# Selective scan with C repeated by DMA and read on GpSimd, and weight splits spread over scan, gap and even cross groups

## The chip, the cores and the metric

The kernel runs on one core of one Trainium2 chip. The time is the device time of one execution in microseconds. Engines: PE is TensorE (PEld its weight loads), DVE is VectorE, ACT is ScalarE, POOL is GpSimd, SP is SyncE, whose queue issues all DMAs here. They run side by side and wait for one another through semaphores only.

## The reference

A two-layer decoder for x of shape (8, 128, 256). Layer 0: attention, a long convolution with ctx, a quantised feed-forward. Layer 1: a selective scan, a stage of self and cross attention with fp8 rounding ("cross" below), and a mixture of experts. The change touches the scan, cross and the start of the experts:

```python
# scan: D_STATE = 16
dt_x, B, C = split(einsum('bld,ed->ble', x, Wx), [64, 16, 16])
dt = softplus(einsum('blr,dr->bld', dt_x, Wdt) + bdt)
dA = exp(einsum('bld,dn->bldn', dt, -exp(A_log)))
dBx = einsum('bld,bln,bld->bldn', dt, B, x)
h = dA_t * h + dBx_t                       # over the 128 positions
y_t = einsum('bdn,bn->bd', h, C_t)         # sum over the 16 states
x = x + y + x * D
# cross: q, k, v, qx = fp8 linears of LN(x), per-head LN of q, k, qx
core = gqa(q, k, v);  xout = gqa(qx, kx, vx)   # kx, vx from ctx
x = x + einsum('bsi,oi->bso', fp8(concat(core, xout) / smooth), wproj) * scale
# experts: silu(h @ gate) * (h @ up) @ down, 16 routed (top 4) and a shared one
```

## The kernel before, in words

Each stage (`begin, attention, convolution, ffn, scan, cross, experts`) gives every engine a function, and each engine runs these one after another in written order. So an instruction waits for its semaphores and for all that its own queue holds ahead of it.

**Scan.** Channels lie on partitions in two halves c = 0, 1, and 8 x 128 = 1024 positions along the free axis. For each of the 16 states n and each c there is a step i = 2n + c. PE repeats the row B_n over all partitions into two PSUM banks (`spread`, a product with the one-column table `pick`), DVE multiplies it by `dtx` (L1114) and scans (L1118), ACT makes `dA`. The reading state x C_n is made by POOL for c = 0 (L1257, `read[0]`), from a copy of PE's spread of C_n that ACT takes out of PSUM (L1176, `c_copy`), and by DVE for c = 1 (L1123, `read[1]`), straight from PSUM. PE adds the readings up in PSUM by a product with the identity (`accumulate`, L1206).

**Splits.** The weights of cross are split into two float16 parts in chunks of 1024 columns: ACT scales a chunk into a scratch tile and casts it (L1409, L1411), POOL writes the remainder (L1417). All 26 chunks go in the first 26 steps of the scan, one a step: q, qx, k, v, the cross weights `kvx`, ctx and `side` (the output projection).

**Cross.** 32 groups g: two halves of the heads of each of 8 batches, first for the self path (g under 16, `path` 0), then for the cross path. For each group PE projects, turns, scores and mixes; DVE takes the maximum of the scores (`biggest`, L2079), divides, normalises (L2105), scales the output (`smoothed`, L2117) and rounds it to fp8 by three instructions (L2124, L1851, L1852); ACT squares, exponentiates (L2256) and copies (`take_pT` L2264, `take_turned` L2248); POOL takes roots (L2337), and adds and rounds (L2322, L2327). For the next batch ACT takes x (`take_x`, L2218), DVE quantises it (L2072, L1851, L1852), and POOL adds (L2311, `add_x`, in even g) and rounds (L2316, L2317, `round_x`, in odd g).

**Experts.** 56 blocks n (28 for each half of the batches); PE computes gate and up (L2416) and down (L2445), ACT the silu (L2456) and a cast (L2477), DVE the gating (L2463, L2470, L2482). Beside block n the table `beside` puts the splitting of further expert weights, a chunk going DVE (L1633), ACT (L1641), POOL (L1648). Blocks 0 to 2 are projected at the end of cross.

Of the kernel before, what the change touches and what calls it, by code (L numbers as in the profile page):

```python
# [1004 lines left out]
def scan(k):  # L1005
# [9 lines left out]
    c_copy = A.take([N])  # L1015
# [5 lines left out]
    unsplit = [A.take([k.proj.SPLIT]), k.XN[:, 0:k.proj.SPLIT // D, :].rearrange("p b d -> p (b d)")]  # L1021
    A = Arena(k.arena, 15080)
# [8 lines left out]
    dt_rows = state[1]  # L1031
# [20 lines left out]
    c_psum = k.sem("sc_c_psum")  # L1052
# [3 lines left out]
    c_taken = k.sem("sc_c_taken")  # L1056
# [9 lines left out]
    def home(n, c):  # L1066

        return 2 * ((n + c) % 2)

    def sync(sp):  # L1070
        sp.wait_ge(k.x_done, 2)
        for dst, src in ((wx, a["Wx"].rearrange("(c p) n -> p c n", p=P)), (wdt[0:DTR], a["Wdt"]),
# [3 lines left out]
            sp.dma_start(dst, src).then_inc(w_loaded, 16)  # L1076

    def vector(dve, link):
# [16 lines left out]
        dve.wait_ge(low_psum, 2)  # L1095
        rows = banks(6)[R0:R1, :]
# [14 lines left out]
        for i, (n, c) in enumerate(STEPS):  # L1111
            product = banks(home(n, c))
# [35 lines left out]
    def scalar(act, link):  # L1148
# [15 lines left out]
        for i, (n, c) in enumerate(STEPS):  # L1164
# [6 lines left out]
            if i < len(w.chunks):  # L1171
                w.split_scalar(act, i, unsplit[i % 2])
            if c:
                act.wait_ge(c_psum, n + 1)
                wait(act, read0_ready, n)
                act.copy(c_copy, banks(home(n, 0))).then_inc(c_taken, 1)  # L1176

    def tensor(pe):
# [63 lines left out]
    def gpsimd(pool, link):  # L1242
# [19 lines left out]
class Projections:  # L1262
# [12 lines left out]
    def __init__(self, k):  # L1275
        self.k = k
        self.base, at = {}, 0
        for m in ("q", "k", "v", "qx"):
# [483 lines left out]
def cross(k):  # L1762
# [544 lines left out]
    def gpsimd(pool, link):  # L2307
# [39 lines left out]
        for g in range(NG):  # L2347
# [4 lines left out]
            if g:  # L2352
                add_c(g - 1)
# [344 lines left out]
```

## Time and profile before

| | before |
|---|---|
| median of 3 runs | 1060.62 us (1060.58 to 1063.05) |
| profiled execution, its own time | 1060.6 us |
| its span | 1058.6 us |
| PE, DVE busy | 86%, 76% of the span |
| ACT, POOL busy | 65%, 49% |
| mean granted TensorE clock | 0.953 |

The 2.0 us between the span and the execution's time lie outside the profile. Busy shares are means over stages of different kinds: the scan lies at 265 to 396 us, cross at 404 to 824, the experts after that. "Granted clock" is the share of 2.4 GHz that TensorE was given; its two levels are 1.2 and 2.4 GHz.

### The profile page before, as it was taken

Reading aid. Unit: us, or ns where it says so; the run is one execution under the profiler, and the core shown is the slowest. Engines: PE = TensorE matmul, PEld = TensorE weight load, DVE = VectorE, ACT = ScalarE, POOL = GpSimd, SP = SyncE. Lnnn points to the kernel's source line nnn. Section 1 sums busy time; section 2 is a strip of 40 time slices with the busy share of each in tenths; the row PEclk is TensorE's granted clock in tenths of the full one; section 3 lists DMA queues with packets and bytes.
Section 4 is the critical chain, followed back from the end, with each engine's and each line's share of the span. In section 5 each row is a group of like instructions: output and inputs, shape, how many; then the busy total and the mean of one; then the engine's idle time right before and its main releaser. Section 6 shows DMA issues by size and latency. Waiting matters only on the chain.

```text
span 1058.6 us, 16127 instructions
## 1 busy us (share of the span) xinstructions
PE 908.1 (86%) x5420; PEld 576.5 (54%) x5420; DVE 805.6 (76%) x1360; ACT 685.0 (65%) x1601; POOL 520.1 (49%) x407
## 2 busy tenths in 40 slices
PE   6898899565667665789899999999999898999998
PEld 3565544233222222566677777777777465655665
DVE  4578889897999998778888777777877766654554
ACT  2656479787989834788886877887776355532232
POOL 3322346351687732568778666677665543400000
PEclk9899899898799997989999999999999899999999
DMA  9832205000000000000000060140003321212121
GB/s 327 334 138 89 72 6 173 9 0 1 0 1 0 0 1 0 1 1 2 1 1 14 28 177 21 41 138 1 2 1 97 124 61 52 70 66 90 67 67 42
DMA packets 36391, 61.32 MB, mean 58 GB/s; under 512 B 5107, under 2 KB 25011, under 8 KB 34773
## 3 DMA queue, kind: packets, MB, share of 16 engines
q1 hardware_dynamic: 36308, 60.30, 16.9%
q8 instruction: 43, 0.70, 0.3%
q14 instruction: 40, 0.32, 0.1%
HBM read 59.17 MB, written 1.12 MB: 57 GB/s over the span
## 4 chain that ended last, share of the span: by engine, by line
PE 48%; DVE 22%; issue 11%; ACT 10%; POOL 6%; DMA 2%; SPq 0%; DVEq 0%; ACTq 0%; POOLq 0%
PE ps L2416 12%; PE ps L2445 6%; DVE arena L1118 4%; DVE ps L1114 3%; PE ps L1944 3%; PE ps L1977 3%; ACT ps L2256 3%; PE ps L1961 2%; PE ps L1990 2%; PE ps L451 2%; PE ps L1951 2%; DVE arena L1123 2%; POOL arena L2337 2%; PE ps L1936 2%; POOL arena L2322 1%
## 5 line engine op out<-in xcount | busy, mean ns | idle before, releaser
L2337 POOL TENSOR_TENSOR arena<-arena 128x4 f32<-128x4 f32 x96 | 98.7, 1028 | 45.5 <-DVE arena L2100 42.9
L2463 DVE TENSOR_TENSOR arena<-ps,arena 128x512 f32<-128x512 f32 (+1 forms) x56 | 38.6, 690 | 89.8 <-ACT ps L2456 89.8
L2256 ACT ACTIVATE ps<-ps,arena 128x128 f32<-128x128 f32 x256 | 89.1, 365 | 22.9 <-DVE arena L2079 22.9
L2248 ACT ACTIVATE arena<-ps,ones 128x512 f32<-128x512 f32 x96 | 68.1, 785 | 48.9 <-PE ps L1951 48.9
L2456 ACT ACTIVATE ps<-ps,arena 128x512 f32<-128x512 f32 (+1 forms) x56 | 36.9, 660 | 89.2 <-PE ps L2416 89.0
L2416 PE MATMUL ps<-XT,wide 128*128 128x512 f16 (+1 forms) x384 | 92.4, 379 | 0.9 <-DVE arena L2482 0.9
L2445 PE MATMUL ps<-wide,arena 128*128 128x256 f16 (+1 forms) x672 | 83.5, 275 | 0.1
L2079 DVE TENSOR_REDUCE arena<-ps 128x4 f32<-128x512 f32 x64 | 43.7, 689 | 50.7 <-PE ps L1961 50.7
L1944 PE MATMUL ps<-wide,arena 128*128 128x512 f16 x256 | 67.1, 398 | 15.4 <-ACT arena L2248 8.9
L2445 PEld LDWEIGHTS ps<-wide,arena 128*128 128x128 f16 (+3 forms) x672 | 65.9, 99 | 20.8 <-issue 1.8
L1961 PEld LDWEIGHTS ps<-arena 128*128 128x128 f32 x512 | 68.5, 195 | 10.3 <-ACT arena L2248 1.2
L1118 DVE TENSOR_TENSOR_SCAN arena<-arena,ps 128x1024 f32<-128x1024 f32 x32 | 73.2, 2287 | 1.1
L1198 PE MATMUL ps<-arena,skip 96*128 96x512 bf16 x96 | 32.0, 418 | 47.9 <-DVE arena L1118 34.9
L1990 PE MATMUL ps<-side,arena 128*128 128x256 f16 x512 | 71.1, 273 | 0.0
L1206 PE MATMUL ps<-arena,ident 128*128 128x512 f32 x128 | 68.2, 660 | 2.6 <-POOL arena L1257 2.6
L1961 PE MATMUL ps<-arena 128*128 128x128 f32 x512 | 68.7, 278 | 0.7 <-ACT arena L2248 0.7
L2327 POOL TENSOR_TENSOR arena<-arena 128x1024 bf16<-128x1024 f32 x32 | 68.2, 2132 | 0.2
L1977 PE MATMUL ps<-arena 128*128 128x256 f32 x256 | 66.7, 384 | 0.9 <-ACT arena L2264 0.9
L2105 DVE TENSOR_TENSOR arena<-ps,arena 128x512 f32<-128x512 f32 x96 | 60.6, 683 | 0.0
L2256 ACT ACTIVATION_READ_ACCUMULATOR ps<-ps,arena 128x1 f32 x256 | 59.3, 232 | 0.0
L1990 PEld LDWEIGHTS ps<-side,arena 128*128 128x128 bf16 x512 | 50.0, 98 | 15.4 <-issue 0.2
L1375 POOL TENSOR_TENSOR wide<-wide,head_mean 128x1024 f32<-128x1024 f32 x12 | 22.7, 1896 | 72.1 <-DVE head_mean L1370 72.1
(343 smaller groups left out, 2405.9 us busy)
## 6 DMA issues: line engine op xcount, KB each, us to landing
arena<-comb_rows SPq DMA_DIRECT2D x26, 256.0 KB, 3.1
side<-in_wproj SPq DMA_DIRECT2D x4, 1024.0 KB, 5.4
arena<-in_w_down SPq DMA_DIRECT2D x7, 512.0 KB, 3.8
wide<-in_w_down SPq DMA_DIRECT2D x1, 3584.0 KB, 15.9
side<-in_w_gate SPq DMA_DIRECT2D x1, 3520.0 KB, 19.5
side<-in_w_up SPq DMA_DIRECT2D x1, 3520.0 KB, 12.4
wide<-in_w_gate SPq DMA_DIRECT2D x2, 1728.0 KB, 12.7
side<-in_w_up SPq DMA_DIRECT2D x3, 1024.0 KB, 9.2
```

Of the source, the lines that this page charges most:

```text
L1118: dve.tensor_tensor_scan(state[c], dA[c], product, 0.0, ALU.mult, ALU.add).then_inc(state_ready, 1)
L1206: last = pe.matmul(ps[:, 4 + 2 * c + j, :], k.ident[:, :], read[i % 2][:, 512 * j:512 * j + 512], start=(n == 0), stop=(n == NST - 1), ski ...
L1944: last = pe.matmul(ps[:, bank, :], x[:, c * S:(c + 1) * S], rhs, start=(i == 0), stop=(i == len(steps) - 1))
L1961: last = pe.matmul(ps[:, 4 + t, i * P:(i + 1) * P], tt[:, MAXB + h, :], tt[:, h // 2, :], start=(i == 0), stop=True, skip_group_check=True)
L1977: last = pe.matmul(ps[:, 4 + t, 2 * i * P:(2 * i + 2) * P], val[g % 2][:, 2 * t + i, :], flat(pT[t][:, 2 * i:2 * i + 2, :]), start=(i == 0 ...
L1990: last = pe.matmul(ps[:, 7, 0:D], cq[g % 2][:, i, :], w.parts(k.side, ((2 * path + half) * QH + i) * D)[part][:, 0:D], start=(half == 0 an ...
L2248: act.activation(flat(turned[g % 2][:, MAXB * j:MAXB * j + MAXB, :]), ps[:, j, :], ACT.Identity, scale=wt[:, 0:1], bias=wt[:, 1:2]).then_i ...
L2256: last = act.activation(ps[:, 4 + t, i * P:(i + 1) * P], ps[:, 4 + t, i * P:(i + 1) * P], ACT.Exp, bias=mx[:, t, i:i + 1], accum_out=den[: ...
L2327: pool.tensor_tensor(flat(cq[g % 2]), flat(cs), flat(cm[g % 2]), ALU.subtract).then_inc(cq_ready, 1)
L2337: pool.tensor_tensor(rs[:, j, :], var[:, j, :], minus_half[:, j, :], ALU.pow).then_inc(rs_ready, 1)
L2416: last = pe.matmul(self.ps[0:m, 2 * up + n % 2, :], y[:, c, :], x[:, c, :], start=(t == 0), stop=(t == len(steps) - 1))
L2445: last = pe.matmul(self.out(b), x[0:m, b * S:(b + 1) * S], y[0:m, :], start=(j == 0 and b % 2 == 0 and t == 0), stop=(j == MC - 1 and t == 2),
```

## The change

1. Scan: C_n no longer goes through PE, PSUM and ACT. SP stores the 16 rows of C to memory once, and then loads each of them repeated over 128 partitions into two tiles `c_rows`. POOL makes both readings; DVE makes the very last one alone. B's banks are fixed by c.
2. Splits: one chunk per state number in the loop, 15 in all. Five more (`TAIL`) go into the gap between scan and cross, three of them on ACT at the scan's end and two after ACT's first `take_x`; PE's first projection waits for these 20. The last six are split in cross in groups 2, 4, ..., 12, on ACT ahead of `take_turned`, on POOL between `round_c` and `add_x`, with one scratch tile.
3. Start of cross: batch 1's `take_x` and quantising go behind the first `take_turned` and all normalising of group 0, and POOL's part behind `root(1, 0)`.
4. Experts: each chunk two blocks later; `turn_comb` and `take_comb` of the second half two blocks later. In cross ACT's `square_piece` and `high_part` come ahead of `take_turned`.

```diff
 def sync(sp):    # scan
+    k.load_cross_small(sp)
+    sp.wait_ge(low_ready, 2)
+    sp.dma_start(rows_dram, dt_rows[R0 + NST:R1, :]).then_inc(c_moved[1], 16)
+    sp.wait_ge(c_moved[1], 16)
+    for n in range(NST):
...
+        wait(sp, read1_ready, n - 1)
+        sp.dma_start(c_rows[n % 2], rows_dram[n:n + 1, :].broadcast_to([P, N])).then_inc(c_moved[n % 2], 16)
 def vector(dve, link):
         for i, (n, c) in enumerate(STEPS):
-            product = banks(home(n, c))
+            product = banks(2 * c)
...
-            if c:
-                dve.wait_ge(state_ready, i + 1)
-                dve.wait_ge(c_taken, n + 1)
-                wait(dve, summed, 2 * n - 1)
-                dve.tensor_tensor(read[1], state[1], banks(home(n, 0)), ALU.mult).then_inc(read1_ready, 1)
+        dve.wait_ge(c_moved[1], 16 * (NST // 2 + 1))
+        dve.wait_ge(state_ready, len(STEPS))
+        dve.wait_ge(summed, len(STEPS) - 2)
+        dve.tensor_tensor(read[1], state[1], c_rows[1], ALU.mult).then_inc(read1_ready, 1)
-        dve.wait_ge(w.split, len(w.chunks))
+        dve.wait_ge(w.split, w.IN_LOOP)
 def scalar(act, link):
-            if i < len(w.chunks):
-                w.split_scalar(act, i, unsplit[i % 2])
-            if c:
-                act.wait_ge(c_psum, n + 1)
-                wait(act, read0_ready, n)
-                act.copy(c_copy, banks(home(n, 0))).then_inc(c_taken, 1)
+            if c == 0 and n < w.IN_LOOP:
+                w.split_scalar(act, n, unsplit[n % 2])
+        act.wait_ge(read1_ready, w.IN_LOOP)
+        for i in range(w.IN_LOOP, w.IN_LOOP + 3):
+            w.split_scalar(act, i, (unsplit[0], c_rows[0])[i % 2])
 def tensor(pe):
         for n in range(NST):
-            if n:
-                accumulate(2 * n - 1)
-            pe.wait_ge(state_ready, 2 * n + 1)
-            spread(n, NST, home(n, 0), c_psum)
             if n:
                 accumulate(2 * n - 2)
             if n + 1 < NST:
+                pe.wait_ge(state_ready, 2 * n + 1)
+                spread(n + 1, 0)
+            if n:
+                accumulate(2 * n - 1)
+            if n + 1 < NST:
                 pe.wait_ge(state_ready, 2 * n + 2)
-                spread(n + 1, 0, home(n + 1, 0), b_psum)
-                pe.wait_ge(read1_ready, n + 1)
-                pe.wait_ge(c_taken, n + 1)
-                spread(n + 1, 0, home(n + 1, 1), b_psum)
+                spread(n + 1, 1)
 def gpsimd(pool, link):
-        for i, (n, c) in enumerate(STEPS):
-            if i < len(w.chunks):
-                w.split_pool(pool, i, unsplit[i % 2])
-            if c == 0:
-                pool.wait_ge(c_taken, n + 1)
-                pool.wait_ge(state_ready, i + 1)
-                wait(pool, summed, 2 * n)
-                pool.tensor_tensor(read[0], state[0], c_copy, ALU.mult).then_inc(read0_ready, 1)
+        for i, (n, c) in enumerate(STEPS[:-1]):
+            if c:
+                w.split_pool(pool, n, unsplit[n % 2])
+            else:
+                pool.wait_ge(c_moved[n % 2], 16 * (n // 2 + n % 2 + 1))
+            pool.wait_ge(state_ready, i + 1)
+            wait(pool, summed, i - 1)
+            pool.tensor_tensor(read[c], state[c], c_rows[n % 2], ALU.mult).then_inc((read0_ready, read1_ready)[c], 1)
+        for i in range(w.IN_LOOP, w.IN_LOOP + w.TAIL):
+            w.split_pool(pool, i, (unsplit[0], c_rows[0])[i % 2])
 # Moe
-        self.beside = {n: ([("in", n + self.EARLY - 1)] if 0 < n <= self.CHUNKS - self.EARLY else [])
-                       + ([("down", n // 2 + 1)] if n % 2 == 0 and n < MC - 2 else []) for n in range(MC)}
+        self.beside = {n: ([("in", n + 3)] if self.EARLY <= n + 3 < self.CHUNKS else [])
+                       + ([("down", n // 2)] if n % 2 == 0 and 0 < n < MC else []) for n in range(MC)}
 # cross, tensor(pe), ahead of project(0, 0), and in group 15
-        pe.wait_ge(w.split, len(w.chunks))
+        pe.wait_ge(w.split, w.IN_LOOP + w.TAIL)
+            if g + 1 == 2 * B:
+                pe.wait_ge(w.split, len(w.chunks))
 # cross, scalar(act)
         take_x(0)
+        k.last_splits(act)
         square(0, 0)
...
-        take_x(1)
...
+        take_x(1)
         for g in range(NG):
...
-            if nxt:
-                for j in range(3):
-                    take_turned(g + 1, j)
+            if g in later:
+                w.split_scalar(act, w.IN_LOOP + w.TAIL + later.index(g), unsplit, 1)
             if g in squaring:
                 moe.square_piece(act, squaring.index(g))
             if g in beside:
                 moe.high_part(act, beside.index(g))
+            if nxt:
+                for j in range(3):
+                    take_turned(g + 1, j)
```

What stands in ACT's queue from the last steps of the scan to the first group of cross, before (L2218 is `take_x`, L2248 `take_turned`, L2227 and L2232 the squares of the projections):

```order
L1176 COPY arena<-ps 128x1024
L175 ACT_TABLE_LOAD
L175 ACTIVATE std<-mv,eps 128x1
L2218 ACTIVATE arena<-ps,ones 128x128 x4
L2227 ACTIVATE arena<-ps 128x128 x4
L175 ACTIVATE std<-mv,eps 128x7
L2232 ACTIVATE arena<-ps 128x4x128
L2218 ACTIVATE arena<-ps,ones 128x128 x8
L2232 ACTIVATE arena<-ps 128x4x128
L2239 ACTIVATE arena<-ps,ones 128x512
```

And now (L1430 and L1432 are a split's two instructions, L2247 is `take_x`, L2277 `take_turned`):

```order
L1430 ACTIVATE arena<-wide,ranged 128x1024
L1432 CAST wide<-arena 128x1024
L175 ACT_TABLE_LOAD
L175 ACTIVATE std<-mv,eps 128x1
L2247 ACTIVATE arena<-ps,ones 128x128 x4
L1430 ACTIVATE arena<-wide,factor 128x1024
L1432 CAST wide<-arena 128x1024
L1430 ACTIVATE arena<-wide,factor 128x1024
L1432 CAST wide<-arena 128x1024
L2256 ACTIVATE arena<-ps 128x128 x4
L175 ACTIVATE std<-mv,eps 128x7
L2261 ACTIVATE arena<-ps 128x4x128 x2
```

Two of the splits stand between the first `take_x` and the first squares, three ahead of the table load, and the second `take_x` has moved down, behind three `take_turned`.

POOL's queue from the middle of an even group of cross (g = 4) on, before (L2337 roots, L2327 `round_c`, L2311 `add_x`, L2333 and L2337 the next group's first root, L2322 `add_c`):

```order
L2337 TENSOR_TENSOR arena<-arena 128x4 x2
L2327 TENSOR_TENSOR arena<-arena 128x1024
L2311 TENSOR_TENSOR arena<-arena 128x1024
L2333 TENSOR_TENSOR arena<-arena,flip 128x4
L2337 TENSOR_TENSOR arena<-arena 128x4
L2322 TENSOR_TENSOR arena<-arena 128x1024
```

And now (lines shifted by 32; L1438 is the split):

```order
L2369 TENSOR_TENSOR arena<-arena 128x4 x2
L2359 TENSOR_TENSOR arena<-arena 128x1024
L1438 TENSOR_TENSOR wide<-arena,wide 128x1024
L2343 TENSOR_TENSOR arena<-arena 128x1024
L2365 TENSOR_TENSOR arena<-arena,flip 128x4
L2369 TENSOR_TENSOR arena<-arena 128x4
L2354 TENSOR_TENSOR arena<-arena 128x1024
```

Where two instructions of 1024 columns stood one after the other there are now three.

ACT's queue at the start of the experts, before (L2456 silu, L2477 cast of the hidden block, L1641 cast of a weight chunk):

```order
L2456 ACTIVATE ps<-ps,arena 128x512
L1641 CAST wide<-arena 128x512
L2477 CAST arena<-ps 128x512
L1641 CAST wide<-arena 128x512 x2
L1641 CAST side<-arena 128x512
L1641 CAST wide<-arena 128x512
L2456 ACTIVATE ps<-ps,arena 128x512
```

And now:

```order
L2490 ACTIVATE ps<-ps,arena 128x512
L1663 CAST wide<-arena 128x512
L2511 CAST arena<-ps 128x512
L1663 CAST wide<-arena 128x512
L2490 ACTIVATE ps<-ps,arena 128x512
L2511 CAST arena<-ps 128x512
```

The silu of block 3 (the last L2456, now the last L2490) had four chunk casts ahead of it behind the hidden block's cast; now it has one.

## Rows read from the trace of the kernel before

**Rows 1.** Busy time by stretch: start:end, length, PE, PEld, DVE, ACT, POOL, clock, DMA.

```profile
265.00:396.00 131.00, 89.12 (x212) 30.87 (x212) 129.13 (x81) 103.54 (x99) 91.73 (x42) 0.89 0.00 0
...
471.00:571.00 100.00, 91.60 (x616) 69.00 (x615) 87.64 (x146) 80.28 (x289) 78.91 (x61) 1.00 0.00 1
```

**Rows 2.** Timeline of the scan loop, DVE: start us, us, engine, line, operation.

```profile
317.58 1.21 DVE L1114 TENSOR_TENSOR ps<-arena,ps 128x1024 f32<-128x1024 f32 x1
...
321.14 1.22 DVE L1123 TENSOR_TENSOR arena<-arena,ps 128x1024 f32<-128x1024 f32 x1
...
322.28 1.22 DVE L1114 TENSOR_TENSOR ps<-arena,ps 128x1024 f32<-128x1024 f32 x1
...
325.74 1.21 DVE L1114 TENSOR_TENSOR ps<-arena,ps 128x1024 f32<-128x1024 f32 x1
```

**Rows 3.** POOL's reading and split by line: ns min/median/max, first and last start.

```profile
L1257 POOL TENSOR_TENSOR arena<-arena x16: 2345/2360/2370, 270.9 to 394.1; 128x1024 f32<-128x1024 f32 x16
...
L1417 POOL TENSOR_TENSOR wide<-XN,wide x8: 2121/2127/2133, 273.2 to 331.2; 128x1024 f16<-128x1024 f32 x8
```

**Rows 4.** Timeline of the scan's last state number, PE, one `accumulate`.

```profile
392.01 1.88 PE L1206 MATMUL ps<-arena,ident 128*128 128x512 f32 x4
```

**Rows 5.** DMA issues: count, KB each, median us to landing.

```profile
arena<-comb_rows SPq DMA_DIRECT2D x26, 256.0 KB, 3.1
...
arena<-in_ln_ffn SPq DMA_DIRECT2D x1, 512.0 KB, 6.3
```

**Rows 6.** Timeline at the scan's end.

```profile
388.84 2.29 DVE L1118 TENSOR_TENSOR_SCAN arena<-arena,ps 128x1024 f32<-128x1024 f32 x1
...
394.06 2.35 POOL L1257 TENSOR_TENSOR arena<-arena 128x1024 f32<-128x1024 f32 x1 [6.19 <-PE ps L1206]
...
400.13 1.40 DVE L1133 SCALAR_TENSOR_TENSOR XN<-XT,arena,ps 128x512 f32<-128x512 f32 x2
```

**Rows 7.** Timeline of one split on ACT.

```profile
312.54 1.14 ACT L1409 ACTIVATE arena<-wide,ranged 128x1024 f32<-128x1024 f32 x1
...
313.71 1.05 ACT L1411 CAST wide<-arena 128x1024 f16<-128x1024 f32 x1
```

**Rows 8.** Timeline of the start of cross.

```profile
404.67 1.50 ACT L2218 ACTIVATE arena<-ps,ones 128x128 bf16<-128x128 f32 x4 [1.36 <-PE ps L1917]
...
408.21 1.23 DVE L2064 TENSOR_TENSOR arena<-arena 128x1024 f32<-128x1024 bf16 x1
...
410.91 5.09 PE L1944 MATMUL ps<-wide,arena 128*128 128x512 f16 x12 [6.33 <-DVE arena L2067]
...
416.26 2.90 ACT L2218 ACTIVATE arena<-ps,ones 128x128 bf16<-128x128 f32 x8 [1.14 <-PE ps L1917]
...
426.55 0.69 DVE L2079 TENSOR_REDUCE arena<-ps 128x4 f32<-128x512 f32 x1 [4.17 <-PE ps L1961]
```

**Rows 9.** Timeline in the feed-forward: POOL and DVE together.

```profile
219.66 2.34 POOL L997 TENSOR_TENSOR arena<-XT,arena 128x1024 f32<-128x1024 f32 x1
...
219.98 2.04 DVE L831 TENSOR_TENSOR arena<-arena 128x5 f32<-128x5 f32 x1
```

**Rows 10.** Timeline of an even group of cross.

```profile
515.29 2.12 ACT L2248 ACTIVATE arena<-ps,ones 128x512 f32<-128x512 f32 x3 [2.02 <-PE ps L1951]
515.67 2.32 POOL L2311 TENSOR_TENSOR arena<-arena 128x1024 f32<-128x1024 bf16 x1
...
516.05 2.23 DVE L1851 TENSOR_SCALAR arena<-arena 128x1024 uint16<-128x1024 uint16 x1
...
518.65 0.68 DVE L2079 TENSOR_REDUCE arena<-ps 128x4 f32<-128x512 f32 x1
```

**Rows 11.** Timeline of the start of the experts.

```profile
838.25 0.65 ACT L2456 ACTIVATE ps<-ps,arena 128x512 f32<-128x512 f32 x1
...
840.43 2.72 PE L2416 MATMUL ps<-XT,side 128*128 128x512 f16 x6 [3.61 <-DVE arena L2482]
...
847.36 1.46 PE L2416 MATMUL ps<-XT,side 128*128 128x512 f16 x6
```

More of the change, by code:

```diff
@@ L1014, in scan @@
     dA = [A.take([N]) for _ in range(2)]
-    c_copy = A.take([N])
+    c_rows = [A.take([N])]
     state = [A.take([N]) for _ in range(2)]
@@ L1021, in scan @@
     unsplit = [A.take([k.proj.SPLIT]), k.XN[:, 0:k.proj.SPLIT // D, :].rearrange("p b d -> p (b d)")]
+    c_rows.append(A.take([N]))
+    assert A.at <= 15080, A.at
+    rows_dram = k.nc.dram_tensor("scan_rows", (NST, N), F32, kind="Internal").ap()
     A = Arena(k.arena, 15080)
@@ L1030, in scan @@
     w = k.proj
-    dt_rows = state[1]
+    dt_rows = c_rows[1]
     R0, R1 = DTR, DTR + 2 * NST
@@ L1051, in scan @@
     b_psum = k.sem("sc_b_psum")
-    c_psum = k.sem("sc_c_psum")
+    c_moved = [k.sem(f"sc_c_moved{i}") for i in range(2)]
     dA_ready = k.sem("sc_dA_ready")
@@ L1093, in scaled @@
             link(dve.tensor_tensor(dtx[:, c, :], dt[:, c, :], k.XT[:, c, :], ALU.mult))
-        dve.wait_ge(low_psum, 2)
-        rows = banks(6)[R0:R1, :]
+        dve.wait_ge(low_ready, 2)
+        rows = dt_rows[R0:R1, :]
         link(dve.tensor_copy(high, rows))
@@ L1193, in tensor, with spread @@
             last.then_inc(dt_psum, 1)
-        def spread(n, first, bank, done):
+        def spread(n, c):
             for j in range(2):
-                last = pe.matmul(ps[:, bank + j, :], pick[0:K3, first + n:first + n + 1].broadcast_to([K3, P]), parts[0:K3, 512 * j:512 * j + 512],
+                last = pe.matmul(ps[:, 2 * c + j, :], pick[0:K3, n:n + 1].broadcast_to([K3, P]), parts[0:K3, 512 * j:512 * j + 512],
                                  start=True, stop=True)
-            last.then_inc(done, 1)
+            last.then_inc(b_psum, 1)
         def accumulate(i):
@@ L1307, in __init__, with of @@
         self.centring += [self.kvx[:, c, 0:G * HD] for c in range(KC)]
-        self.chunks = [(k.wide, self.base[m] + c * self.COLS[m] + n, self.factor[:, c, j:j + 1])
-                       for j, m in enumerate(self.ORDER) for c in range(KC)
-                       for n in range(0, self.COLS[m], self.SPLIT)]
+        def of(*names):
+            return [(k.wide, self.base[m] + c * self.COLS[m] + n, self.factor[:, c, j:j + 1])
+                    for j, m in enumerate(self.ORDER) if m in names for c in range(KC)
+                    for n in range(0, self.COLS[m], self.SPLIT)]
+        half = NQ * D
+        self.chunks = of("q", "k", "v")
+        self.chunks += [(k.side, n, self.ranged[:, 6:7]) for n in range(0, half, self.SPLIT)]
+        self.FIRST = len(self.chunks)
+        self.chunks += [(self.ct, n, self.ranged[:, 5:6]) for n in range(0, KC * B * S, self.SPLIT)]
         self.chunks += [(k.wide, n, self.ranged[:, 4:5])
                         for n in range(self.kvx_at, self.kvx_at + KC * 2 * G * HD, self.SPLIT)]
-        self.chunks += [(self.ct, n, self.ranged[:, 5:6]) for n in range(0, KC * B * S, self.SPLIT)]
-        self.chunks += [(k.side, n, self.ranged[:, 6:7]) for n in range(0, 2 * NQ * D, self.SPLIT)]
+        self.chunks += of("qx")
+        self.chunks += [(k.side, half + n, self.ranged[:, 6:7]) for n in range(0, half, self.SPLIT)]
     def raw(self, m, c):
@@ L1407, in split_scalar @@
         tensor, at, scale = self.chunks[i]
-        wait(act, self.split, i - 1)
+        wait(act, self.split, i + 1 - buffers)
         act.mul(tmp, tensor[:, at:at + self.SPLIT], scale).then_inc(self.scaled, 1)
@@ L1808, in cross @@
     beside = range(19, 19 + moe.EARLY)
+    later = range(2, 2 + 2 * (len(w.chunks) - w.IN_LOOP - w.TAIL), 2)
+    unsplit = k.arena[:, moe.weights_at:moe.weights_at + w.SPLIT]
     squaring = (12, 14, 16, 18, 19, 20, 21)
@@ L1891, in sync @@
         moe.load_small(sp, w_loaded)
+    k.load_cross_small = load_small
+    def sync(sp):
         sp.wait_ge(xq_ready, B)
@@ L2345, in gpsimd @@
             root(0, j)
-        add_x(1)
         for g in range(NG):
-            if g == 0:
-                round_x(1)
             if g + 1 < NG:
                 root(g + 1, 0)
+            if g == 0:
+                add_x(1)
+                round_x(1)
             if g:
@@ L2358, in gpsimd @@
                 round_c(g - 1)
+            if g in later:
+                w.split_pool(pool, w.IN_LOOP + w.TAIL + later.index(g), unsplit)
             if g % 2 == 0 and 0 < g and (g + 4) // 2 < B:
```

33 lines of the change are left out of this document (19 added, 14 removed).

## Prediction

> **What bounds the kernel now.** I read the stretches first [rows 1]. From 265 to 396 us, the scan, DVE is busy 129.13 of 131 us, PE 89, ACT 104, POOL 92: DVE sets the pace and nothing waits for the others. In cross (471 to 571) no engine is full: PE 91.60, DVE 87.64, ACT 80, POOL 79 of 100, so an order of work decides there which wait counts. The timeline of the loop [rows 2] shows one state number as 325.74 - 317.58 = 8.16 us: the step c = 1 takes 322.28 - 317.58 = 4.70 (it holds DVE's reading, 1.22) and c = 0 takes 3.46. Then I read the four places where the change puts a queue in another order: the scan's end [rows 6], the start of cross [rows 8], an even group [rows 10] and the first blocks of the experts [rows 11]. The profiled execution took 1060.6 us, 2.0 more than its span; the median is 1060.62, so sums against the one hold for the other.
>
> **Loop.** DVE loses its reading and both steps become alike: 2 x 3.46 = 6.92 instead of 8.16 us, 1.24 less for 15 state numbers: **-18.6 us**. What has to keep up:
> - POOL takes both readings and a split: 2 x 2.36 + 2.13 = 6.85 us [rows 3], 99% of 6.92. It just fits; the two readings of a state number may lag some 2 us before DVE must wait for a state buffer. I take nothing for it, and for a bad case 0.3 us of hand-over in each n (7.2 us): +4.5.
> - PE has two accumulates of 1.88 [rows 4] and four spread products: about 5 of 6.92. Its two spreads of C go. At half clock (the loop's mean is 0.89) some n would take nearly double, about 10; before, such stretches stood in the loop too and DVE stayed at 129 of 131.
> - ACT loses the copy of C (1.0 us) and about half of the splits (1.14 + 1.05 [rows 7]): not a bound.
> - C arrives by DMA, 512 KB repeated over the partitions, with two tiles. The trace has no such load of a row during the scan; the nearest are 256 KB landing in 3.1 us and 512 KB in 6.3 us, that one queued behind others [rows 5]. A tile is asked for again when its second reading ends, so two state numbers take one landing + about 0.4 + 6.85 us; against 2 x 6.92 the landing is hidden up to about 6.5 us. I take 3 to 6.3: nothing.
>
> **Scan's end.** State 30 is ready at 388.84 + 2.29 = 391.13; the sums end at 400.13 + 1.40 = 401.53, 10.4 us later, since POOL's last reading began only at 394.06, behind PE's accumulate [rows 4, 6]. Now POOL reads at once (to +2.4), splits (to about +4.5), DVE reads state 31 at +3.4 or, if it must wait for that split, at +4.5 (done +5.7), PE adds to +7.6, and the last sum ends at +8.35: **-2.0** (-3.0 without the wait).
>
> Why I reckon with that wait: a DVE operation of 128x5 with two SBUF inputs took 2.04 us while POOL worked on 128x1024, from 219.98 to 222.02, POOL's ending at 222.00 [rows 9]; and in the even group DVE's rounding (L1851) took 2.23 us to 518.28, over POOL's addition, which ended at 517.99 [rows 10]. So each holds the other off until its whole instruction ends. In the loop DVE's multiply and scan take one input from PSUM, and they kept their 1.21 and 2.29 us beside POOL's readings [rows 2, 6]; more readings on POOL cost them nothing. The Trainium skill ("SBUF — State Buffer", section "Who interferes with whom") states the same: an operation of VectorE with two SBUF inputs, or in a 2-port mode, and one of GpSimd that reads SBUF exclude each other for the whole instruction. By that rule, the trace agrees, 2.04 us; the sum by it is the one below, and were it not so, the waits at both ends and in the even groups would fall away, some 12.8 us more gain.
>
> **Start of cross.** ACT's first `take_x` ends at 404.67 + 1.50 = 406.17; two splits behind it (1.14 + 1.05 each, [rows 7]) end at 410.6. POOL's two remainders (2.13 each) and DVE's three two-input operations (the first at 408.21 to 409.44) hold each other off in turn, so the last split ends near 415.1, where PE's projection, which now waits for it, began at 410.91 [rows 8]: +4.2 (without holding off 412.8: +1.9). The second `take_x` (2.90 us) and its quantising leave the way of group 0, but enter it again behind `take_turned`, in front of the first maxima; these come +4.5 later than at 426.55, and I take **+4.8** for the whole start.
>
> **Even groups.** At g = 4 `round_c` ends and `add_x` runs from 515.67 to 517.99; DVE's L1851 stands waiting from 516.05, and the first maximum of the next group begins at 518.65, 0.37 after L1851 [rows 10]. Now a split of 2.13 runs in `add_x`'s place and `add_x` behind it: L1851 waits for the one, L1852 for the other. The maximum begins near 520.5: +1.9. That for g = 2, 4, ..., 10 gives **+9.5**. On ACT the split (1.14 + 1.05 = 2.19) falls into an idle time of 2.02 before `take_turned` [rows 10], 0.2 late, hidden behind the same POOL work; at g = 12 a piece of squaring of some 1.1 us also comes ahead: 2.19 + 1.1 - 2.02, **+0.8** with roundings, where no `add_x` stands.
>
> **Experts.** At 838.25 the silu comes behind four chunk casts, so PE idles 3.61 us until 840.43, and then runs at half clock: six products take 2.72 us there, 1.46 later [rows 11]. With the chunks two blocks later PE goes on near 836.7: 3.7 earlier, and the low clock not set off, some 2.5 us over the products that ran slow: **-6.2**.
>
> **Sum:** -18.6 - 2.0 + 4.8 + 9.5 + 0.8 - 6.2 = -11.7; the first step of the loop, ahead of these 15, also loses the way of C through PE and ACT, which I put at -0.4 by choice: 1060.6 - 12.1 = **1048.5 us**.
>
> **Rivals.**
> - A, the sum: 1048.5. Its own range is 1044 to 1052 (no holding off at the two ends: 1045.2; half clock in the experts as before: 1051). Chance 0.47.
> - B, the even groups cost nothing: were the scaled output ready only 0.5 us later, L1851 would start behind POOL, and DVE has slack in cross (87.64 of 100). For it: PE is the fuller engine there. Against it: the maximum stood directly behind L1852 with no wait [rows 10]. 1048.5 - 9.5 = 1039. Chance 0.20.
> - C, POOL bounds the loop: 99% leaves no room for 0.3 us a state number [rows 3]. 1053. Chance 0.17.
> - D, slower: C lands late. One row of memory read 128 times may be slower than the loads that I have rows for [rows 5]. From 6.5 us landing on every us costs 0.5 us per state number; at about 9 us these take 8.13 and the whole gain of the loop is lost, and the ends and cross stay: 1060.6 - 0.4 + 4.8 + 9.5 + 0.8 - 2.0 - 6.2 = about 1067. It ends above 1060.6 from some 8.2 us landing. Chance 0.06.
> - E, slower: PE idles more in cross (+4.8, +1.9 in each even group, where it was busy 91.60 of 100 at clock 1.00 [rows 1]), and its clock falls after such an idle stretch as it did after 3.61 us [rows 11]. An episode costs some 2.5 us by that case; in all six groups of the late splits 15: 1063. It decides from five episodes on. For it: idle of 6.33 at the start of cross [rows 8] grows. Against: an idle of 1.9 is half of 3.61. Chance 0.10.
>
> **How the numbers follow.** What can be told from no change is 0.3%, 3.2 us: 1057.4 to 1063.8. The likeliest is A: 1048.5. The range reaches from B with a little more (1038) to C with a few us of E (1057); below it and above it I leave about 0.18 in all, D and E mostly. Faster: A, B, C, and the mild end of E, 0.85; same 0.07 and slower 0.08 from D and E.
>
> **What the changed profile would show.** Right: L1122 starts 6.9 us apart for equal c, DVE without idle times in the loop, POOL near 98% busy there; the sums' last operation 8.4 us after state 30; PE's first projection near 4 us later counted from the scan's end; in groups 2 to 10 two DVE roundings of about 2 us, each ending with a POOL instruction; the experts' block 3 without an idle time over 1 us and at clock 1. Wrong: idle times of L1122 released by POOL (C) or POOL's released by the C loads with landings above 6.5 us (D); roundings of 0.43 us in even groups (B); granted clock below 1 in cross where it was 1.00 (E). The prediction fails first if the even groups' +9.5 or the loop's -18.6 is mis-sized; these two carry its sign and size.

## The result and the profile after

The changed kernel takes 1047.49 us (median of 4, 1047.01 to 1048.04), against 1060.6 for the kernel before on the same chip: ratio 0.9873, 95% interval 0.9856 to 0.9891. The forecast was 1048.5, with a range of 1038 to 1057. Its profiled execution took 1048.04 us, with a span of 1046.2.

Where the 12.4 us of span went can be read from a few instructions that both profiles have. The times of such marks, and their distances:

| from ... to | before | after | change | forecast |
|---|---|---|---|---|
| start to the first L1122 (L1114) | 265.14 | 265.45 | +0.3 | 0 |
| to the last L1122 | 125.90 | 106.84 | -19.1 | -19.0 |
| state 30 ready to the last sum (L1140) | 10.40 | 8.49 | -1.9 | -2.0 |
| last L1122 to group 1's first maximum | 47.45 | 49.96 | +2.5 | +2.8 |
| group 1 to group 12 | 141.85 | 152.50 | +10.7 | +9.5 |
| group 12 to group 13 | 11.27 | 12.33 | +1.1 | +0.8 |
| group 13 to group 31 | 220.94 | 219.19 | -1.75 | 0 |
| group 31's first maximum to the end | 246.05 | 239.93 | -6.1 | -6.2 |

The fourth line holds the third: at the start of cross itself +4.4, where +4.8 was forecast. Of the 4.4, 3.2 lie ahead of group 0's first maximum and 1.2 between it and group 1's (11.94 us before, 13.15 after). The first maxima of the groups (L2079, now L2108) are the marks in cross; counted by them, the even group of [rows 10] is group 6, not 4 as the prediction calls it, which changes no number.

The loop. Timeline of DVE in the changed kernel, which answers to [rows 2]:

```profile
310.27 1.21 DVE L1122 TENSOR_TENSOR ps<-arena,ps 128x1024 f32<-128x1024 f32 x1
311.51 2.29 DVE L1126 TENSOR_TENSOR_SCAN arena<-arena,ps 128x1024 f32<-128x1024 f32 x1
313.71 1.21 DVE L1122 TENSOR_TENSOR ps<-arena,ps 128x1024 f32<-128x1024 f32 x1
...
317.16 1.21 DVE L1122 TENSOR_TENSOR ps<-arena,ps 128x1024 f32<-128x1024 f32 x1
```

A state number takes 317.16 - 310.27 = 6.89 us. Busy times of the loop, columns as in [rows 1]:

```profile
265.00:376.00 111.00, 72.96 (x183) 27.25 (x184) 109.77 (x66) 69.15 (x65) 104.76 (x47) 0.95 0.19 67
```

DVE stays the bound (109.77 of 111 us), POOL is close behind (104.76 us, and it starts only at 269.14). The DMA of C, from the page of the profile:

```profile
arena<-scan_rows SPq DMA_DIRECT2D x16, 512.0 KB, 3.6
```

The scan's end and the start of cross, timeline of POOL and DVE:

```profile
374.83 7.31 POOL L1438 TENSOR_TENSOR wide<-arena,wide 128x1024 f16<-128x1024 f32 x3
...
375.91 2.14 DVE L1130 TENSOR_TENSOR arena<-arena 128x1024 f32<-128x1024 f32 x1
...
379.27 1.60 DVE L1140 SCALAR_TENSOR_TENSOR XN<-XT,arena,ps 128x512 f32<-128x512 f32 x2
...
387.52 5.30 POOL L1438 TENSOR_TENSOR wide<-arena,wide 128x1024 f16<-128x1024 f32 x2 [5.38 <-ACT wide L1432]
...
388.63 2.22 DVE L2095 TENSOR_TENSOR XT<-arena 128x256 bf16<-128x256 f32 x1
390.77 2.87 DVE L2096 TENSOR_TENSOR arena<-arena 128x768 bf16<-128x768 f32 x1
...
393.79 5.05 PE L1971 MATMUL ps<-wide,arena 128*128 128x512 f16 x12 [10.06 <-DVE arena L2096]
```

DVE's last reading took 2.14 us beside POOL's splits (1.22 alone, as a run below shows), its L2095 and L2096 2.22 and 2.87, where the same two took 0.42 and 0.95 before. POOL's two splits took 5.30 us instead of 4.25: the two engines held each other off, in turn. No semaphore of the kernel stands between these operations, so the sentence ahead of the prediction that engines wait for one another "through semaphores only" doesn't hold for DVE and POOL. PE's projection came 0.15 us behind L2096, 0.97 behind the splits.

An even group (6), timeline of DVE and POOL, which answers to [rows 10]:

```profile
504.20 0.44 DVE L2153 TENSOR_SCALAR arena<-arena 128x1024 bf16<-128x1024 bf16 x1
504.67 2.24 DVE L1875 TENSOR_SCALAR arena<-arena 128x1024 uint16<-128x1024 uint16 x1
506.94 2.23 DVE L1876 TENSOR_SCALAR arena<-arena 128x1024 bf16<-128x1024 bf16 x1
509.10 1.28 DVE L2108 TENSOR_REDUCE arena<-ps 128x4 f32<-128x512 f32 x2
...
504.32 2.31 POOL L1438 TENSOR_TENSOR side<-arena,side 128x1024 f16<-128x1024 f32 x1
506.59 2.30 POOL L2343 TENSOR_TENSOR arena<-arena 128x1024 f32<-128x1024 bf16 x1
```

The two roundings end at 506.91 and 509.17, just behind the split's end (506.63) and the addition's (508.89). So L1875 waited for the rest of the split, and L1876 for the whole addition.

TensorE's clock in cross. Two windows of this profile, group 2 and group 5; columns as in [rows 1], where the clock is the last number but two:

```profile
440.70:455.30 14.60, 14.60 (x93) 10.95 (x92) 12.07 (x16) 10.79 (x34) 11.80 (x8) 0.93 0.01 2
482.10:495.50 13.40, 11.41 (x66) 8.32 (x64) 10.48 (x21) 11.49 (x40) 9.71 (x9) 0.87 0.00 1
```

The same two groups in a second profile of the same kernel, the first run of the next section:

```profile
440.50:454.10 13.60, 13.60 (x94) 10.40 (x93) 12.07 (x17) 10.68 (x34) 12.08 (x9) 1.00 0.01 2
480.80:494.00 13.20, 10.54 (x72) 7.90 (x71) 11.60 (x22) 11.38 (x40) 10.61 (x10) 1.00 0.01 1
```

Group 2 took 14.64 us at clock 0.93 and 13.58 at 1.00, group 5 13.44 at 0.87 and 13.16 at 1.00. In group 5 the clock was at 0.50 from 487.2 to 490.6 us; PE's timeline ahead of it has no longer idle times than these:

```profile
485.28 0.66 PE L1996 MATMUL ps<-ident,arena 128*128 128x128 f32 x4 [1.19 <-DVE arena L2118]
...
487.17 1.11 PE L1996 MATMUL ps<-ident,arena 128*128 128x128 f32 x4 [0.80 <-DVE arena L2118]
```

The start of the experts, which answers to [rows 11], has no idle time and full clock:

```profile
833.42 1.46 PE L2450 MATMUL ps<-XT,wide 128*128 128x512 f16 x6
834.71 1.46 PE L2450 MATMUL ps<-XT,side 128*128 128x512 f16 x6
836.01 1.47 PE L2479 MATMUL ps<-wide,arena 128*128 128x256 f16 x12
```

### The profile page after: what moved, and what is told of

Same layout as the page of the kernel before. It is cut to its first block, busy times and chain, and to the rows that moved or that the text cites. A ratio compares the mean times of both kernels' runs of the same rounds, so it can differ in the third digit from the quotient of the medians.

```text
span 1046.2 us, 16036 instructions
## 1 busy us (share of the span) xinstructions
PE 896.8 (86%) x5388; PEld 578.0 (55%) x5388; DVE 801.4 (77%) x1345; ACT 672.7 (64%) x1585; POOL 558.8 (53%) x422
## 4 chain that ended last, share of the span: by engine, by line
PE 30%; POOL 22%; DVE 21%; issue 18%; ACT 5%; DMA 2%; SPq 0%; POOLq 0%; DVEq 0%; ACTq 0%
PE ps L2450 10%; POOL arena L2354 6%; POOL arena L2369 6%; DVE arena L1126 6%; POOL arena L2359 6%; PE ps L2479 5%; DVE ps L1122 4%; PE ps L451 2%; DMA wide<-in_w_down 1%; PE ps L491 1%; PE ps L727 1%; PE ps L729 1%; PE ps L728 1%; PE ps L484 1%; POOL arena L2349 1%
## 5 line engine op out<-in xcount | busy, mean ns | idle before, releaser
L2490 ACT ACTIVATE ps<-ps,arena 128x512 f32<-128x512 f32 (+1 forms) x56 | 36.9, 659 | 82.1 <-PE ps L2450 82.1
L2277 ACT ACTIVATE arena<-ps,ones 128x512 f32<-128x512 f32 x96 | 68.0, 780 | 28.9 <-PE ps L1978 28.9
L1267 POOL TENSOR_TENSOR arena<-arena 128x1024 f32<-128x1024 f32 x31 | 72.9, 2353 | 21.3 <-DVE arena L1126 19.2
L1971 PE MATMUL ps<-wide,arena 128*128 128x512 f16 x256 | 67.0, 398 | 18.6 <-DVE arena L2096 10.1
L2108 DVE TENSOR_REDUCE arena<-ps 128x4 f32<-128x512 f32 x64 | 43.3, 687 | 41.5 <-PE ps L1988 41.3
L2004 PE MATMUL ps<-arena 128*128 128x256 f32 x256 | 70.7, 402 | 0.9 <-ACT arena L2293 0.9
L1218 PE MATMUL ps<-arena,ident 128*128 128x512 f32 x128 | 61.8, 605 | 2.8 <-POOL arena L1267 1.6
L1175 ACT ACTIVATE arena<-arena 128x1016 f32<-128x1016 f32 x32 | 36.5, 1142 | 39.0 <-DVE arena L1126 39.0
## 6 DMA issues: line engine op xcount, KB each, us to landing
wide<-in_w_gate SPq DMA_DIRECT2D x2, 1728.0 KB, 13.6
```

Of the source, the lines that this page charges most:

```text
L1267: pool.tensor_tensor(read[c], state[c], c_rows[n % 2], ALU.mult).then_inc((read0_ready, read1_ready)[c], 1)
L1971: last = pe.matmul(ps[:, bank, :], x[:, c * S:(c + 1) * S], rhs, start=(i == 0), stop=(i == len(steps) - 1))
L2004: last = pe.matmul(ps[:, 4 + t, 2 * i * P:(2 * i + 2) * P], val[g % 2][:, 2 * t + i, :], flat(pT[t][:, 2 * i:2 * i + 2, :]), start=(i == 0 ...
L2277: act.activation(flat(turned[g % 2][:, MAXB * j:MAXB * j + MAXB, :]), ps[:, j, :], ACT.Identity, scale=wt[:, 0:1], bias=wt[:, 1:2]).then_i ...
```

## The experiments

The profiles begin the scan loop at 263.6 to 268.1 us, ahead of all that the runs below change. So spans are compared from the loop's first multiply (L1122) on, called "from the loop on": 793.5 us before, 780.75 after. Such sums come from one profile of each kernel. In the edits, `...` stands for lines that are left out, and a line with # names the place. The changed kernel was run again beside others:

> The changed kernel once more, unchanged, beside the two others of this call: the profiles of different calls begin the scan loop at 263.6 to 266.8 us, ahead of everything that the change touches, so differences are counted from there. Expected: 780.8 us from the first L1122 to the end of the span, as in its first profile, within 0.5.

It took 1048.41 us (ratio 0.9901, interval 0.988 to 0.9922), 780.5 from the loop on. Differences below of 0.5 us or less are not told from none. Single stretches of cross differ by more: from group 1 to group 12 this profile took 151.50 us where the first took 152.50. The low clock moved: group 2 took 13.58 us at 1.00 (14.64 at 0.93 in the first), group 11 12.87 us at 0.87 (11.90 at 1.00).

**Where the late splits stand.**

```diff
-    later = range(2, 2 + 2 * (len(w.chunks) - w.IN_LOOP - w.TAIL), 2)
+    later = (12, 13, 14, 15, 16, 17)
 # tensor, group 15
-                pe.wait_ge(w.split, len(w.chunks))
+                pe.wait_ge(w.split, w.IN_LOOP + w.TAIL + 2)
 # tensor, project_out
+            if g == 2 * B and first == 0:
+                pe.wait_ge(w.split, len(w.chunks))
```

> The changed kernel, with its six late splits in groups 12 to 17 instead of 2, 4, ..., 12; nothing is left out. My theory: each split in groups 2 to 10 cost 1.6 to 2.9 us (measured 10.0 together, 1.1 more at group 12), since VectorE's two roundings L1875 and L1876 are held off one after the other by the split and the addition; from group 12 on no addition stands there and TensorE is the full engine (12.0 us of 12), so most of it goes: 1047.5 - 9 = 1038.5, 1037 to 1041. Rival: the split's time on POOL and ACT has to be paid wherever it stands: 1046 to 1048. In the profile: L1876 0.43 us in groups 2 to 10.

1040.65 us, ratio 0.982 (0.9806 to 0.9835); 775.0 from the loop on, -5.8. Groups 2 to 11 fell from 122.15 to 112.63 us (before: 111.58), -9.5, nearly all of their cost. The same group in this run, DVE:

```profile
500.81 2.23 DVE L1875 TENSOR_SCALAR arena<-arena 128x1024 uint16<-128x1024 uint16 x1
503.07 0.43 DVE L1876 TENSOR_SCALAR arena<-arena 128x1024 bf16<-128x1024 bf16 x1
503.42 0.68 DVE L2110 TENSOR_REDUCE arena<-ps 128x4 f32<-128x512 f32 x1
```

But groups 12 to 18 took 86.59 instead of 83.24: +3.35 came back, as at the new places the splits weren't hidden entirely (groups 13 to 17 between 0.3 and 1.0 us each). The theory held for what is removed; that TensorE hides all of it later did not.

**POOL's share against ACT's.**

```diff
+        if self.IN_LOOP + self.TAIL <= i < len(self.chunks) - 1:
+            pool.wait_ge(self.proj_loaded, 64 + 16 * (i - self.IN_LOOP - self.TAIL + 1))
+            lo, tmp, hi = lo[:, 0:64], tmp[:, 0:64], hi[:, 0:64]
         pool.tensor_tensor(lo, tmp, hi, ALU.subtract).then_inc(self.split, 1)
...
 # cross, sync
+        for i in range(w.IN_LOOP + w.TAIL, len(w.chunks) - 1):
+            sp.wait_ge(w.scaled, 2 * i + 2)
+            hi, lo = w.parts(*w.chunks[i][0:2])
+            sp.dma_start(lo, hi).then_inc(w.proj_loaded, 16)
```

> The changed kernel, but POOL's part of the splits in groups 2 to 10 works on 64 columns of 1024, and the rest of the low part is a DMA copy of the high part (so the low parts of these five chunks are left out); ACT's part stays where it is. It tells POOL's share from ACT's. My theory: POOL's split alone is what costs, by holding VectorE off: of 10.0 us 9 go, 1047.5 - 9 = 1038.5, with L1876 at 0.43 us. Rival: ACT's two instructions ahead of take_turned are the cost: no change, 1047.5.

This kernel leaves out the low parts of five chunks. It took 1039.53 us, ratio 0.9809 (0.9796 to 0.9822); 771.5 from the loop on, -9.3. The ACT part stayed, so it is not the cost. The run isn't clean in one point: POOL waited for the copy, so the addition came later too, and both roundings took 0.43 us.

```profile
501.46 0.43 DVE L1878 TENSOR_SCALAR arena<-arena 128x1024 uint16<-128x1024 uint16 x1
501.92 0.43 DVE L1879 TENSOR_SCALAR arena<-arena 128x1024 bf16<-128x1024 bf16 x1
...
503.21 0.31 POOL L1441 TENSOR_TENSOR side<-arena,side 128x64 f16<-128x64 f32 x1 [2.07 <-DMA side<-side]
503.48 2.12 POOL L2350 TENSOR_TENSOR arena<-arena 128x1024 f32<-128x1024 bf16 x1
```

The even group 6 took 11.3 us so, against 13.6 after and 12.0 before: the wait of [rows 10] went as well. Odd groups gave 0.3 to 1.2 back.

**POOL's last two splits of the gap, moved.**

```diff
 # scan, gpsimd
-        for i in range(w.IN_LOOP, w.IN_LOOP + w.TAIL):
+        for i in range(w.IN_LOOP, w.IN_LOOP + 3):
...
 # cross, gpsimd, behind root(0, j)
+        for i in range(w.IN_LOOP + 3, w.IN_LOOP + w.TAIL):
+            w.split_pool(pool, i, (k.tail_scratch, unsplit)[i % 2])
 # tensor, ahead of project(0, 0)
-        pe.wait_ge(w.split, w.IN_LOOP + w.TAIL)
+        pe.wait_ge(w.split, w.IN_LOOP)
 # scalar, in group 0 ahead of take_pT
+            if g == 0:
+                act.wait_ge(w.split, w.IN_LOOP + w.TAIL)
```

The second of the two has another scratch tile, too.

> The changed kernel, with POOL's part of the last two splits in the gap moved behind its third root of group 0, where it was idle 6.3 us, and TensorE's first projection waiting for 15 splits instead of 20; nothing is left out. My theory: these two splits held off VectorE's L2095 and L2096 (2.22 and 2.87 us instead of 0.42 and 0.95), which gave all of TensorE's 3.7 us delay: 1047.5 - 3.7 = 1043.8. Rival: the wait for the splits themselves is the price and something else of the start is late next, or the late start is caught up in groups 1 and 2: 1046 to 1047.5. In the profile: L2095 0.42, L2096 0.95, the first projection 3.7 us earlier.

1044.61 us, ratio 0.9861 (0.9846 to 0.9876); 778.0 from the loop on, -2.8. At the start all came as expected, with the splits on ACT where they were:

```profile
387.82 0.42 DVE L2097 TENSOR_TENSOR XT<-arena 128x256 bf16<-128x256 f32 x1
388.16 0.95 DVE L2098 TENSOR_TENSOR arena<-arena 128x768 bf16<-128x768 f32 x1
...
396.94 3.21 DVE L157 TENSOR_SCALAR XN<-X,mv,rstd 128x256 f32<-128x256 f32 x4
...
397.88 4.25 POOL L1439 TENSOR_TENSOR wide<-arena,wide 128x1024 f16<-128x1024 f32 x2
```

From the last L1122 the projection came 3.7 us earlier, and the rest of the start took part of it back. At the new place the splits hold off DVE's L157 (3.21 us, before 1.38).

**Both.** The two edits together:

> Both edits of the two runs before it together; nothing is left out. My theory: they act at different places and add up: 1047.5 - 9 - 3.7 = 1034.8, 1033 to 1038. Rival: TensorE or another engine bounds cross by then, and the sum is less than the two.

1037.98 us, ratio 0.9795 (0.9781 to 0.9808); 771.7 from the loop on, -9.0, the sum of -5.8 and -2.8 within what can be told. It is the fastest kernel here, with the one that follows. That one moves POOL's second split of the two once more:

```diff
 # cross, gpsimd
-        for i in range(w.IN_LOOP + 3, w.IN_LOOP + w.TAIL):
-            w.split_pool(pool, i, (k.tail_scratch, unsplit)[i % 2])
+        w.split_pool(pool, w.IN_LOOP + 3, k.tail_scratch)
 # behind root(1, 2)
+            if g == 0:
+                w.split_pool(pool, w.IN_LOOP + w.TAIL - 1, unsplit)
...
```

> The run with both edits (1038.0, 771.7 us from the first L1122), with POOL's last split of the gap put behind the roots of group 1, where POOL idles 5.2 us and VectorE reads PSUM, instead of behind the first one. My theory: the two splits there held off VectorE's L157 (3.21 us instead of 1.38) and with it the third normalising; one alone holds it off less: -1.0 to -1.8 by the first maximum, 1036.5. Rival: the maximum hangs on another chain by then and nothing moves: 1038.

1037.99 us, ratio 0.981 (0.9785 to 0.9834); 771.5: nothing. L157 took 3.20 us all the same: one split alone was enough to hold it off. The theory for this step fell.

**POOL's room in the loop.**

```diff
+    extra = A.take([256])
...
                 w.split_pool(pool, n, unsplit[n % 2])
+                wait(pool, read1_ready, n)
+                pool.tensor_tensor(extra, dt[:, 0, 0:256], dt[:, 1, 0:256], ALU.mult)
```

> The changed kernel, with one more POOL product of 256 columns per state number in the scan loop (its result is used by nothing). My theory: POOL's work of 2 x 2.36 + 2.13 = 6.85 us a state number just fits into VectorE's 6.89, so an addition of about 0.65 us makes POOL the bound: 7.50 us a state number, 15 x 0.6 = +9, 1056.5, with idle times before L1122 that POOL ends. Rival: POOL has hidden slack there (its readings run ahead or behind), and nothing moves: 1047.5.

1054.91 us, ratio 0.9973 (0.9961 to 0.9986); 788.1 from the loop on, +7.3. The loop took 113.4 us instead of 106.84. In its second half:

```profile
317.49 2.17 POOL L1441 TENSOR_TENSOR wide<-arena,wide 128x1024 f16<-128x1024 f32 x1
319.58 0.76 POOL L1265 TENSOR_TENSOR arena<-arena 128x256 f32<-128x256 f32 x1
...
324.90 2.16 POOL L1441 TENSOR_TENSOR wide<-XN,wide 128x1024 f16<-128x1024 f32 x1
```

7.41 us a state number, POOL without a gap, and DVE's scan waits for the reading: over the window 270 to 380, from the waits:

```profile
DVE arena L1127 <- POOL arena L1270: 7.0, 13, 0.6
```

13 waits of 0.54 us. The extra product holds POOL for 320.26 - 319.58 = 0.68 us of the 7.41 (its next reading starts at 320.26), so the rest takes POOL 6.73 of DVE's 6.89: 0.2 us of room a state number. The first 2 of the 15 state numbers were free, as the readings could first fall behind: 15 would have cost 7.7 us, the loop lost 6.5.

**Twice the DMA.**

```diff
-            sp.dma_start(c_rows[n % 2], rows_dram[n:n + 1, :].broadcast_to([P, N])).then_inc(c_moved[n % 2], 16)
+            for dst in (extra[n % 2], c_rows[n % 2]):
+                sp.dma_start(dst, rows_dram[n:n + 1, :].broadcast_to([P, N])).then_inc(c_moved[n % 2], 16)
...
```

> The changed kernel, with each row of C loaded twice, the first time into a tile that nothing reads, so that a tile of C is there later. Measured landing of one load: 3.6 us. My theory: two state numbers take landing + 0.4 + 6.85, so the load hides up to a landing of 6.5 us; two loads behind one another land at about 7.2, which gives 7.2 us a state number instead of 6.89: +5, 1052 (1047.5 if the two overlap and land below 6.5). Rival: the loads have far more room, or none: no change, or +10 and more.

1047.6 us, ratio 0.9914 (0.9895 to 0.9933), 781.0 from the loop on, 6.90 us a state number: no change. The page of the profile says why:

```profile
arena<-scan_rows SPq DMA_DIRECT2D x24, 512.0 KB, 4.8
XN<-scan_rows SPq DMA_DIRECT2D x8, 512.0 KB, 3.5
```

The first line mixes the 16 rows that are read with 8 of the others. Load by load, the second of each pair, the one that is read, landed in 4.6 to 5.5 us (median 4.9), issued 0.36 us behind the first: the two overlap and stay below 6.5. The threshold itself was not reached, so it isn't shown.

**VectorE makes half of the readings.**

```diff
 # vector, in the loop
+            if c:
+                dve.wait_ge(c_moved[n % 2], 16 * (n // 2 + n % 2 + 1))
+                dve.wait_ge(state_ready, i + 1)
+                wait(dve, summed, i - 1)
+                dve.tensor_tensor(read[1], state[1], c_rows[n % 2], ALU.mult).then_inc(read1_ready, 1)
...
 # gpsimd, in the loop
             if c:
                 w.split_pool(pool, n, unsplit[n % 2])
+                continue
```

> The changed kernel with VectorE making the reading of c = 1 from the row that DMA brought, POOL only that of c = 0 and the split. It tells what the loop gains from the DMA of C alone and what from POOL taking the reading. My theory: VectorE's reading has two SBUF inputs here, so to its 1.22 us comes a wait for the POOL instruction that is under way: 8.1 to 9.5 us a state number, +18 to +39, so 1066 to 1086. Rival: no holding off: exactly the 8.16 us of before, 1066.

1082.34 us, ratio 1.0216 (1.0189 to 1.0242); some 9.1 us a state number (313.92 to 323.05 for the multiply of one c), slower than before. The reading, by its line (ns, smallest, median, largest):

```profile
L1132 DVE TENSOR_TENSOR arena<-arena x16: 1224/2124/2139, 275.2 to 412.2; 128x1024 f32<-128x1024 f32 x16
```

1.22 us is the operation, 2.12 with POOL's split under way. So the DMA of C gains nothing by itself in this form; read from SBUF on VectorE it even costs some 1.0 us a state number over the read from PSUM (8.16). The gain is POOL's taking the reading.

**The table beside.** With `("in", n + self.EARLY - 1)`, `("down", n // 2 + 1)` and `turn_comb`, `take_comb` at 14 and 15, as before:

> The changed kernel with the table beside and turn_comb, take_comb of before. My theory: TensorE's idle 3.6 us and the half clock behind it at the start of the experts come back: 1047.5 + 6.1 = 1053.6, with the silu of block 3 behind four chunk casts. Rival: the gain of 6.1 us between the last maximum of cross and the end came from elsewhere (from the order in cross): 1047.5 to 1049.

1051.98 us, ratio 0.9953 (0.9938 to 0.9969); 785.9 from the loop on, +5.1, of which 5.2 lie behind group 31 (245.1 us to the end instead of 239.9). The idle time is back:

```profile
833.45 1.48 PE L2450 MATMUL ps<-XT,side 128*128 128x512 f16 x6 [3.62 <-DVE arena L2516]
834.74 2.74 PE L2479 MATMUL ps<-wide,arena 128*128 128x256 f16 x12
```

Fewer products ran slow behind it than in [rows 11] (12 here took 2.74 us, the ones around them 1.48), which accounts for the 0.9 us less.

**ScalarE's order in cross.** `square_piece` and `high_part` moved behind the three `take_turned`, their old place:

> The changed kernel with square_piece and high_part behind take_turned in ScalarE's queue, as they stood before; the late splits stay ahead of it. A gain of 1.75 us between groups 13 and 24 was not in my sum. My theory now: it comes from these two standing ahead of take_turned, in ScalarE's idle time of 2.0 us there, where they had pushed the squares of the next group: +1.75, 1049.2. Rival: the groups from 13 on only caught up because they are bound by TensorE: no change, 1047.5; the intervals of groups 20 to 24 stay 12.00 us and not 12.26.

1047.7 us, ratio 0.992 (0.99 to 0.9939); 781.6 from the loop on, +0.9. The intervals of groups 20 to 22 are 12.28 us again (12.00 after, 12.26 before), +0.84, group 15's 12.48 instead of 12.00; group 12, where a piece stood beside a split, is 0.5 faster. ACT's timeline shows the place in group 21:

```profile
689.77 2.12 ACT L2277 ACTIVATE arena<-ps,ones 128x512 f32<-128x512 f32 x3 [2.02 <-PE ps L1978]
691.77 1.06 ACT L1601 ACTIVATE arena<-arena 128x1024 f32<-128x1024 f32 x1
692.81 0.62 ACT L1663 CAST wide<-arena 128x512 f16<-128x512 f32 x1
```

An idle time of 2.02 us stands ahead of `take_turned` and 1.7 us of work behind it, in front of the next group's squares. Ahead of `take_turned` the work lies in the idle time: there 0.34 us of it are left in the changed kernel.

## Why the prediction was right, step by step

- **Loop, -18.6 - 0.4.** Right in size (-19.1) and cause: two equal steps, DVE the bound, POOL just fitting. The twice-loaded row and the added POOL work show which of the two other bounds is near: POOL, with 0.2 us of room. Rival C had the right mechanism and would have needed only some 0.2 us more. Rival D needed a landing over 6.5 us; it was 3.6. The 0.4 that was put down to the first step is not in the traces: the loop begins 0.3 us later than before (within the spread of these starts), and its first step takes 3.47 us in both. The 15 state numbers alone give 15 x (8.16 - 6.89) = 19.05; 1.24 a state number had been forecast, and it was 1.27.
- **Scan's end, -2.0.** -1.9, and in its steps: DVE's last reading ended 5.67 us after state 30 (forecast 5.7), the sums at 8.49 (8.35).
- **Start of cross, +4.8.** +4.4. The mechanism was right, the last link not: the prediction let PE wait for the last split at +4.2; PE waited for DVE's L2096, held off by those splits, and came 3.7 us later, counted from the end of the first `take_x`. The last split itself was done 0.8 us before L2096. Moving POOL's part away while the ACT part stayed gave all of the 3.7 back there (4.73 us from `take_x` to the projection, 4.74 before, 8.46 after). By group 0's first maximum +3.2 is left, where +4.5 was forecast. The other 1.2, between the first maxima of groups 0 and 1, go with the clock: 11.94 us at 1.00 before, 12.4 at 0.86 in the three runs with the two splits moved, 13.15 at 0.74 here. No run separates that clock from the order of work.
- **Even groups, +9.5.** The whole stretch cost +10.7. A group's split cost 1.6 to 1.8 us in groups 4 to 10 (1.9 forecast), and 2.9 in group 2, of which 1.8 are the split's: at clock 1.00 in the second profile group 2 took 13.58 us against 11.76 before. That makes 8.9 us for the five splits, a little less than the 9.5. The rest goes with the clock, which is rival E's mechanism: 1.06 in group 2 at a granted clock of 0.93, and 0.28 each in groups 5 and 7 at 0.87, where the second profile has these groups at 1.00 and a fall to 0.87 in group 11 instead (+0.97). The loss in group 2 isn't its split's: it stays when the splits are moved away (12.91 us at 0.91). The falls in groups 3 to 11 do come with the splits: each of the eight profiles that have them in the even groups shows one to three, and the profile before, the three with the splits moved and the one with POOL's part cut show none. E was right that the clock would fall, and too dear with 2.5 us an episode. Its argument against itself, that a short idle time might not do it, fails: ahead of the fall at 487.2 us PE had idled 1.19 and 0.80 us. Why the clock fell there and not in the same groups of the second profile stays open. Rival B did not occur in the changed kernel: L1875 stood ready 0.35 us behind the split's start, as L1851 had behind the addition's (0.38). Its time was nearly reached by the run with POOL's part cut.
- **Group 12, +0.8.** +1.06. Group 13 gave 0.47 of it back (11.67 us before, 11.20 after).
- **Groups 13 to 31, 0.** -1.75, the one term that the prediction left out. It named the moved `square_piece` and `high_part` only as a cost at group 12. Put back, they cost +1.3 us in groups 15 and 20 to 22, -0.5 in group 12. The other 0.47 are group 13's, which stayed at 11.20 us in that run; no run says why.
- **Experts, -6.2.** -6.1; the table alone gives 5.2. The difference is how many products run slow behind the idle time (18 before, 12 and some small ones in that run); why, stays open.

That the sum came within 1 us of the median is in part luck, by errors of both signs: +1.2 and +0.3 in cross against -1.75 and -0.4. The low clock, which the sum has at nothing in cross, comes to 1.6 us of the even groups' 10.7 and goes with 1.2 us of the start's 4.4.

## What to carry to other kernels

Before work is moved to GpSimd, look what VectorE does at that moment. Beside the multiply and scan with one operand in PSUM it was free here (1.21 and 2.29 us in both kernels). Beside roundings and additions in SBUF the instruction of the one waited until that of the other had ended, and when both engines had several in a row, each waited for a whole one (2.24 and 2.23 us instead of 0.43). Place such work by the other engine's timeline, not where its own engine idles. Give an engine that is 98% busy in a loop its room in us per round, since the first rounds hide an overload.

Read the same stretch in two profiles of one kernel before a difference of a microsecond is put down to the work in it: the low clock of TensorE moved from group 2 to group 11 between two of them.

Idle time ahead of an instruction in a queue is a place for small work; behind the same instruction it may stand in the next group's way.

## What the runs showed that I had not expected

- A reading on VectorE from two SBUF tiles took 2.12 us beside a split of 2.13 (1.22 alone), so that half of the readings on VectorE made the kernel slower than before.
- Two loads of 512 KB issued together landed in 3.5 and 4.9 us (median), where one alone took 3.6: the second comes 1.3 us later, and not 3.6.
- The granted clock fell to half in cross with no idle time of TensorE above 1.2 us just ahead of it.
- A single split of 2.1 us stretched a group of four VectorE operations of 1.38 us together to 3.20, as much as two did (3.21).
